# A five-layer graph kernel: half-width messages, fewer sorted supers, one-hots made two batches ahead

## The reference

```python
mean = segment_sum(h2[src], dst) / max(cnt, 1)
out  = l2norm(mean @ Wl2 + b + h2 @ Wr2)      # Wl2, Wr2: 128 x 64
out  = l2norm(out + x)
```

## Time and profile before

| what | us |
|---|---|
| median of 3 runs | 9816.29 |
| lowest, highest | 9815.36, 9822.09 |
| the profiled execution, its own time | 9828.25 |
| its span in the trace | 9826.3 |

### The profile page before, as it was taken

The page is one execution under the profiler, slowest core; times in us unless marked ns, Lnnn a source line. Parts: engine busy times, 40 slices in busy tenths (PEclk is TensorE's granted clock), DMA queues, the critical chain, the costliest instruction groups (busy, mean ns, idle before and its releaser), DMA issues.

```text
span 9826.3 us, 131949 instructions
## 1 busy us (share of the span) xinstructions
PE 5787.9 (59%) x31232; PEld 4379.0 (45%) x31233; DVE 3782.0 (38%) x8447; ACT 1893.4 (19%) x4165; POOL 6141.1 (62%) x6486
## 2 busy tenths in 40 slices
PE   4576675556666666688888236666666633333333
PEld 3444454446666666555555223434443422222222
DVE  3355552224444444455555333444444311111111
ACT  1111111111111111122222123333333300000000
POOL 6766557767777777765655324444444357777777
PEclk6555556557777777788888657778778755555555
DMA  3111111123333333355555224444444311111111
GB/s 74 34 28 27 27 27 35 35 47 98 98 97 98 98 98 97 105 136 135 135 132 131 60 84 146 142 144 150 147 149 146 106 38 30 30 30 30 30 30 29
DMA packets 544865, 813.71 MB, mean 83 GB/s; under 512 B 200060, under 2 KB 343256, under 8 KB 544010
## 3 DMA queue, kind: packets, MB, share of 16 engines
q0 software_dynamic: 207424, 296.93, 14.7%
q1 hardware_dynamic: 200459, 408.44, 13.0%
q10 hardware_dynamic: 136191, 99.81, 3.3%
HBM read 706.10 MB, written 98.49 MB: 82 GB/s over the span
## 4 chain that ended last, share of the span: by engine, by line
POOL 37%; PE 16%; issue 15%; DMA 14%; DVE 10%; SPq 5%; ACT 3%; ACTq 1%; DVEq 0%; POOLq 0%
POOL G L832 37%; PE PH L1980 9%; DMA HT<-src_rows 9%; SPq L640 3%; PE NB L1980 3%; PE PAG L1980 2%; DMA GROWS<-h_tab 2%; PE NA L1980 2%; DVE HT L1815 2%; DMA HT<-h_tab 2%; DVE HT L1747 1%; SPq L632 1%; ACTq L884 1%; DVE HT L1764 1%; SPq L742 1%
## 5 line engine op out<-in xcount | busy, mean ns | idle before, releaser
L1980 PE MATMUL PH<-HT 128*128 128x288 bf16 (+6 forms) x12902 | 2494.2, 335 | 1380.9 <-DVE HT L1815 522.9
L1980 PE MATMUL PAG<-OH,G 128*64 128x96 f32 (+2 forms) x9910 | 1519.8, 332 | 1832.9 <-DMA G<-rel_tab,IDX 986.2
L1980 PEld LDWEIGHTS PH<-HT 128*128 128x128 bf16 (+4 forms) x12902 | 1549.1, 152 | 2304.2 <-ACT HT L869 550.5
L1980 PEld LDWEIGHTS PAG<-OH,G 128*64 128x64 f32 (+2 forms) x9910 | 1393.7, 209 | 1951.8 <-issue 1904.8
L832 POOL DMA_INDIRECT G<-in_x,SRC x1525 | 1453.9, 953 | 688.2 <-issue 451.1
L832 POOL DMA_INDIRECT G<-h_tab,SRC x1040 | 984.7, 947 | 1392.0 <-PE PAG L1980 1074.8
L832 POOL DMA_INDIRECT G<-rel_tab,IDX x1507 | 1422.1, 944 | 574.6 <-issue 459.8
L832 POOL DMA_INDIRECT G<-far_tab,SRC x1527 | 1442.2, 944 | 485.0 <-issue 465.3
L1424 DVE TENSOR_TENSOR AGG<-AGG,PAG 128x96 f32 (+2 forms) x832 | 205.9, 247 | 2807.0 <-PE PAG L1980 2801.7
L832 POOL DMA_INDIRECT G<-x_tab,SRC x883 | 837.9, 949 | 534.4 <-PE PAG L1980 270.8
L1980 PE MATMUL PAG<-OH,HT 128*128 128x96 f32 x3126 | 613.3, 377 | 521.4 <-ACT HT L1120 521.4
(11 more groups left out here) (240 smaller groups left out, 4827.8 us busy)
## 6 DMA issues: line engine op xcount, KB each, us to landing
HT<-h_parts SPq DMA_DIRECT2D x150, 937.5 KB
HT<-x_parts SPq DMA_DIRECT2D x210, 468.8 KB
GROWS<-rel_tab SPq DMA_DIRECT2D x4096, 0.2 KB
HT<-src_rows SPq DMA_DIRECT2D x370, 160.0 KB
GROWS<-in_x SPq DMA_DIRECT2D x3584, 0.2 KB
rel_tab<-STG ACTq DMA_DIRECT2D x200, 250.0 KB
GROWS<-far_tab SPq DMA_DIRECT2D x3072, 0.5 KB
GROWS<-rel_tab ACTq DMA_DIRECT2D x3072, 0.2 KB
```

Source lines behind the costliest of these rows:

```text
L1980: return nc.tensor.matmul(dst, lhsT, rhs, start=start, stop=stop, skip_group_check=True)
```

## The change

**Half-width messages.** After layer 2 a pass of its own, `messages`, runs over the 50 units: SyncE loads `hT` (4 buffers), ScalarE applies batch norm and relu, TensorE multiplies by `[Wl2 | Wr2]` (128 x 128) and adds the bias, ScalarE copies the result, ScalarE stores the `Wr2` half (`r_tab`), SyncE stores the `Wl2` half (`g_tab`, 64 columns), VectorE splits that half into three bf16 parts and SyncE stores them (`g_parts`). Layer 3 gathers 64-column rows from `g_tab`, with no shift and no relu, when all stores of `g_tab` and `r_tab` have landed; a unit's first beat has two products with `FOLD` (which adds the two halves of the sums) and adds the row of `r_tab`. `h_tab`, gamma's row and the constant row `CROW_P` are gone.

**Supers.** 64 supers are sorted, over steps 60 to 188 of layer 0, a super in two steps (order and one-hots in one, ranks in the next). Layers 2 and 3 both gather 132 and pick 64 (16 windows, 160 batches), spread evenly over the first 126 steps.

**Buffers.** `PX` has 5 buffers, `SROW` 4, the source one-hots 3, the destination one-hots 4; VectorE makes one-hots two batches ahead, SyncE loads four batches ahead. The wide compare is five compares of 288 f16 columns.

```diff
-CELL_LAYERS = {2: (112, 29), 3: (132, 35)}
+CELL_LAYERS = {2: (132, 35), 3: (132, 35)}
-SORT_STEP = 40
-COUNT_SUPERS = 3 * CELL_SUPERS
+SORT_STEP = 60
+COUNT_SUPERS = 4 * CELL_SUPERS
-WIDTH = {2: PARTS * D, 3: PARTS * H}
-PAIR = {2: 2, 3: 1}
+WIDTH = PARTS * D
+PAIR = 2
-PX_BUFS = {2: 6, 3: 3}
+PX_BUFS, SROW_BUFS = 5, 4
+S_BUFS, D_BUFS = 3, 4
+HOT_AHEAD, LOAD_AHEAD = 2, 4
+HT_BUFS = 4
...
-        due = min(s + 1, head) if s < ramp else min(total, head + -(-(total - head) * (s - ramp + 1) // steps))
+        due = min(total, -(-total * (s + 1) // (supers - 6)))
```

SyncE, with the message pass between the two `load_cells`:

```diff
+            def messages():
+                def load(u):
+                    b = u % HT_BUFS
+                    if u >= HT_BUFS:
+                        sp.wait_ge(msg_hot, u - HT_BUFS + 1)
+                    sp.dma_start(HTB[:, b, :], turned(u)).then_inc(ht_in[b], 16)
+                sp.wait_ge(stored[2], all_stored(2))
+                for u in range(HT_BUFS):
+                    load(u)
+                for u in range(UNITS):
+                    sp.wait_ge(msg_copied, u + 1)
+                    sp.dma_start(rows_of(g_tab, u), MESSAGES[u % 2][0:HALF, :, 0:D]).then_inc(msg_out[u % 2], 16)
+                    if u + HT_BUFS < UNITS:
+                        load(u + HT_BUFS)
+                    sp.wait_ge(msg_split, 4 * u + 4)
+                    sp.dma_start(g_parts[0:HALF, u, :], PARTS_X[0:HALF, u % 2, :]).then_inc(g_parts_out[u % 2], 16)
...
             def load_batch(p, g):
+                b, u = g % PX_BUFS, g % BATCHES * BATCH
+                if p == 3 or g >= PX_BUFS:
+                    sp.wait_ge(cell_picked, pairs_covering(p, g - PX_BUFS))
...
+                b = g % SROW_BUFS
+                if p == 3 or g >= SROW_BUFS:
+                    sp.wait_ge(cell_hot, BATCHES_BEFORE[p] + g - SROW_BUFS + 1)
```

GpSimd before layer 3, and ScalarE:

```diff
-                        pool.wait_ge(stored[2], all_stored(2))
+                        messages_out(pool)
...
+            def messages():
+                def take(u):
+                    rows_ = MESSAGES[u % 2][0:HALF, :, :]
+                    act.wait_ge(msg_made, u + 1)
+                    if u >= 2:
+                        act.wait_ge(msg_out[u % 2], 32 * (u // 2))
+                        act.wait_ge(msg_split, 4 * (u - 1))
+                    copy(rows_, MESSAGE_P[u % 2].rearrange("p (a c) -> p a c", a=2)).then_inc(msg_copied, 1)
+                    act.wait_ge(msg_copied, u + 1)
+                    act.dma_start(rows_of(r_tab, u), rows_[:, :, D:2 * D]).then_inc(msg_out[u % 2], 16)
+                act.wait_ge(bn_ready, 1)
+                for u in range(UNITS):
+                    act.wait_ge(ht_in[u % HT_BUFS], 16 * (u // HT_BUFS + 1))
+                    if u >= 2:
+                        act.wait_ge(msg_made, u - 1)
+                    nc.scalar.activation(POS[:, u % 2 * UNIT:(u % 2 + 1) * UNIT], HTB[:, u % HT_BUFS, :], ACT.Relu,
+                                         bias=BSH[:, 0:1], scale=BSC[:, 0:1]).then_inc(msg_hot, 1)
+                    if u:
+                        take(u - 1)
+                take(LAST)
```

VectorE:

```diff
-                if 0 <= i < SORT_SUPERS:
-                    sort_hot_of(i)
-                if 0 < i <= SORT_SUPERS:
-                    sort_rank_of(i - 1)
+                if 0 <= i < 2 * SORT_SUPERS:
+                    (sort_rank_of if i % 2 else sort_hot_of)(i // 2)
...
+            def messages():
+                for u in range(UNITS):
+                    parts = PARTS_X[0:HALF, u % 2, :].rearrange("p (a c) -> p a c", a=2)
+                    rows_, left = MESSAGES[u % 2][0:HALF, :, 0:D], XS[0:HALF, :, :]
+                    dve.wait_ge(msg_copied, u + 1)
+                    if u >= 2:
+                        dve.wait_ge(g_parts_out[u % 2], 16 * (u // 2))
+                    move(parts[:, :, 0:D], rows_).then_inc(msg_split, 1)
...
+                    nc.vector.tensor_tensor(parts[:, :, 2 * D:3 * D], left, parts[:, :, D:2 * D], ALU.subtract)\
+                      .then_inc(msg_split, 1)
...
-                nc.vector.tensor_tensor(HOT_D[:, g % 3, :, :], IOTA_P.unsqueeze(1).to_broadcast(wide),
-                                        DST_TAB[:, w, u:u + BATCH].unsqueeze(2).to_broadcast(wide), ALU.is_equal)\
-                  .then_inc(cell_hot, 1)
+                for i in range(BATCH):
+                    last = nc.vector.tensor_scalar(HOT_D[:, g % D_BUFS, i, :], COLS_16[:, :], DST_TAB[:, w, u + i:u + i + 1], None,
+                                                   ALU.is_equal)
+                last.then_inc(cell_hot, 1)
...
-                        shift_straight(s, s % SLOTS)
```

TensorE:

```diff
+            def messages():
+                for u in range(UNITS):
+                    pe.wait_ge(msg_hot, u + 1)
+                    if u >= 2:
+                        pe.wait_ge(msg_copied, u - 1)
+                    bank, hot = MESSAGE_P[u % 2], u % 2 * UNIT
+                    for a in range(2):
+                        mm(bank[:, a * H:(a + 1) * H], POS[:, hot + a * HALF:hot + (a + 1) * HALF], wlr2[:, :], a == 0,
+                           False)
+                        last = mm(bank[:, a * H + D:(a + 1) * H], ONES[0:1, 0:HALF], sb2r, False, a == 1)
+                    last.then_inc(msg_made, 1)
...
-                        with_bias(NA[0:HALF, a * D:(a + 1) * D], HB[:, half(a)], wr2[:, :], sb2r)
-                        last = mm(NB[0:HALF, a * D:(a + 1) * D], Z[:, half(a)], wl2[:, :])
+                        last = mm(NB[0:HALF, a * D:(a + 1) * D], Z[:, half(a)], FOLD[:, :])
...
-                if 0 < i <= SORT_SUPERS:
-                    sort_order_of(i - 1)
-                if 1 < i <= SORT_SUPERS + 1:
-                    sort_place(i - 2)
+                if i % 2 and 0 < i < 2 * SORT_SUPERS:
+                    sort_order_of(i // 2)
+                if i % 2 == 0 and 0 < i <= 2 * SORT_SUPERS:
+                    sort_place(i // 2 - 1)
```

More of the change, by code:

```diff
@@ L776, in load_cells @@
+                    ahead = [g for at in BATCHES_AT[p][:s + 1] for g in at][-1] + LOAD_AHEAD
+                    for g in range(loaded_batches, min(ahead + 1, batches_of(p))):
+                        load_batch(p, g)
+                        loaded_batches = g + 1
                     piece = P // 8
@@ L996, in beat3 @@
                     root(3, u, 3, beat - 2)
+                    if beat == 2 and (not isinstance(u, int) or u < LAST):
+                        act.wait_ge(chain[3], u * CHAIN[3] + 1)
+                        act.dma_start(RU[0:HALF, :, :], rows_of(r_tab, unit_of(3, u + 1))).then_inc(ru_in, 16)
                 if beat == 5:
@@ L1878, in cell_layer @@
                 _, by_step, rest, _ = CELL_SCHEDULE[p]
-                m, supers = (D if p == 2 else H), SUPERS_OF[p]
+                supers = SUPERS_OF[p]
                 windows = batches_of(p) // BATCHES
@@ L2095, in sum_straight @@
                 b, landed = (None, None) if p == 1 else row_buffer(p, s)
-                if b is not None and p != 3:
+                if b is not None:
                     pe.wait_ge(row_in[b], landed)
@@ L2322, in sum_cells @@
                     pe.wait_ge(cell_copied, PAIRS_BEFORE[p] + e + 1)
[L2323 to L2324 removed]
+                    for k in range(PAIR):
+                        cell = e * PAIR + k
                         g, i = divmod(cell, BATCH)
@@ L2328, in sum_cells @@
                             pe.wait_ge(window_added, WINDOWS_BEFORE[p] + cell // UNITS)
-                        hot = HOT_D[:, g % 3, i, :]
+                        hot = HOT_D[:, g % D_BUFS, i, :]
                         rows_ = PICKED[:, e % GP_BUFS, k * w:(k + 1) * w]
-                        if p == 2:
-                            mm(WIN_SUM, rows_[:, 0:2 * D], hot, first, False)
-                            last = mm(WIN_SUM[0:D, :], rows_[:, 2 * D:3 * D], hot, False, final)
-                        else:
-                            for part in range(PARTS):
-                                last = mm(WIN_SUM, rows_[:, part * H:(part + 1) * H], hot, first and part == 0,
-                                          final and part == PARTS - 1)
+                        mm(WIN_SUM, rows_[:, 0:2 * D], hot, first, False)
+                        last = mm(WIN_SUM[0:D, :], rows_[:, 2 * D:3 * D], hot, False, final)
                     last.then_inc(cell_summed, 1)
```

383 lines of the change are left out of this document (127 added, 256 removed).

## The result

The changed kernel takes 8769.55 us (median of 4 runs, 8763.57 to 8782.85) beside 9819.19 us of the kernel before on the same chip (4 runs, 9815.36 to 9832.08): a ratio of 0.893, 95% interval 0.8915 to 0.8946. Predicted were 8660 us and a range of 8585 to 8890. The profiled execution took 8782.85 us, its span is 8781.0; so the sum of the prediction (a span of 8670) is 111 us short. Where they are is read by stage.

What follows compares the result with a forecast made beforehand. GpSimd's gathers, one per 1.249 us, were taken as every stage's floor, with 1580 us of waits to win. Terms -217 - 36 + 17 + 122 - 1042 = -1156 from a 9826.3 us span gave 8670, hence 8660; range 8585 to 8890.

Steps and rivals of the forecast that it cites:

- loop of two engines: Stage 0: VectorE's one-hots and ranks, TensorE's placing, then the unit's beat take 13.6 us a sorting step, against 9.7 of gathers.
- the 1042 us of stage 3: Stage 3: forecast gain before the message pass, from 2453.5 us to 1299 of gathers, 25 of waits and 87 at the end.
- Stage 0: Stage 0: sorting work spread over two steps, about 9.0 us a step, under the gathers' 9.7; -217 us, bounds 0 and -235.
- The compares: Stages 2 and 3: 1600 new narrow compares lengthen GpSimd's gathers by 11 ns each; +17 us over both stages.
- Rival (c): Stages 2 and 3: new compares block gathers for their whole length, 1600 x 250 ns = 400 us; 9040 us, chance 0.04.
- It is worth nothing: Five compares for one save VectorE 0.4 us a batch, with no gain because GpSimd sets the pace.
- The message pass: New pass between stages 2 and 3: 2.3 us a unit, TensorE's work the longest part; +122 us with first load and last store.
- Stage 3's waits: Stage 3: 25 us left for waits, as its eight beats a unit have more waits between engines than stage 2's five.
- rival (d): Stages 2 and 3: SyncE's queue, loads behind waits then 16 single-row DMAs, sets the pace; slower, 9975 us, chance 0.02.
- rival (a): Stages 2 and 3: TensorE and the beats set the pace, 11 us a super; 8930 us, chance 0.13.
- loads now have three to four batches of lead: Stage 2: loads get 25 us and more of lead, against waits of 16 us at the longest; 8 us of waits remain.
- The last gap: End of stage 3, before stage 4: 87 us where it was 114.8, since TensorE no longer runs behind.

## Why GpSimd waits in stage 3

The changed kernel's timeline around one such wait (SyncE's issues, then TensorE and GpSimd):

```profile
6085.11 0.26 SPq L749 DMA_DIRECT2D HT<-g_parts  x1
...
6085.42 0.35 SPq L755 DMA_DIRECT2D HT<-src_rows  x1
...
6087.98 5.12 SPq L632 DMA_DIRECT2D GROWS<-g_tab  x16
...
6093.75 2.47 PE L1921 MATMUL PAG<-OH,G 128*64 128x96 f32 x14 [8.00 <-DMA GROWS<-g_tab]
...
6096.81 0.94 POOL L833 DMA_INDIRECT G<-g_tab,SRC  x1 [4.25 <-PE PAG L1921]
```

The last of the 128 single rows of a super are issued behind the loads of a batch, which waited for a buffer. TensorE stands 8.0 us for them, then GpSimd 4.25 us for TensorE. Over the whole run:

```profile
PE PAG L1921 <- DMA GROWS<-g_tab: 114.4, 14, 14.5
DVE HT L1756 <- DMA HT<-src_rows: 110.8, 40, 11.1
```

**Rows first.**

```diff
                 for s in range(SUPERS_OF[p]):
+                    if rows_now and s:
+                        some_rows(p, s * piece, (s + 1) * piece)
                     ...
                         load_batch(p, g)
-                    if (s + 1) * piece <= P * len(SP_SUPERS[p]):
-                        some_rows(p, s * piece, (s + 1) * piece)
```

(`rows_now` is the condition of the two lines taken out; at step 0 the rows stay behind the loads.)

> The changed kernel, but in each step of stages 2 and 3 SyncE issues the 16 single-row transfers ahead of the batch loads in place of behind them. Theory A (GpSimd's 84 us of waits in stage 3 come from rows that are issued late, behind a load that waits for a free buffer): TensorE's waits for the rows fall from 114 us (14 of them) to under 30, GpSimd's waits for sums in stage 3 from 84 to under 30 us, and the stage gets 40-60 us shorter; stage 2 changes by less than 15 us. Theory B (TensorE itself is late in stage 3, and the rows are only where it shows): GpSimd's waits stay between 70 and 100 us and another wait takes the rows' place. A third way: the batch loads now come late, and VectorE waits for source rows; then stage 3 gets longer.

**The lookahead of before.**

```diff
-PX_BUFS, SROW_BUFS = 5, 4
-S_BUFS, D_BUFS = 3, 4
-HOT_AHEAD, LOAD_AHEAD = 2, 4
+PX_BUFS, SROW_BUFS = 5, 2
+S_BUFS, D_BUFS = 2, 3
+HOT_AHEAD, LOAD_AHEAD = 1, 2
```

> The changed kernel with the lookahead of before: one-hots one batch ahead (not two), loads two (not four), two buffers for source rows (not four), two for source one-hots (not three), three for destination one-hots (not four). Five buffers of parts stay. The prediction gave the lookahead the credit for the loads' slack. If that is right, VectorE waits for source rows for some 200-400 us again (678 before, 111 in the changed kernel) and GpSimd's waits for sums grow in stages 2 and 3 from 85 us to 200-500 us. If the narrower messages alone did it (a batch of 3.6 us of TensorE's work where it had 6.0), the span grows by less than 40 us.

With the rows first the span was 8746.6 us, 34 less than the changed kernel, nearly all of it in stage 3 (1362.0 us for 1394.1). What waits were left in stage 3, and over the run those for single rows and for source rows:

```profile
POOL G L836 <- PE PAG L1924: 57.9, 22, 9.1
...
PE PAG L1924 <- DMA GROWS<-g_tab: 1.5, 1, 1.5
...
DVE HT L1759 <- DMA HT<-src_rows: 197.6, 69, 10.7
```

TensorE's waits for the rows went from 114.4 us (14) to 1.5 (1), but GpSimd's only from 83.9 to 57.9. Between the two theories: the rows were one cause, of 26 to 34 us; the rest stays when they are on time. TensorE is busy for 166 of the 200 us from 6400 to 6600 in that run, but VectorE now waits 198 us for source rows (111 in the changed kernel), and its later work waits behind that. The runs of the section on a version of the parts speak against TensorE's own work as the cause of the last 58 us: with rows first, the bias on VectorE and one-hots one batch ahead in stage 3, GpSimd waits 18.6 and 25.3 us there, while TensorE's busy time is nearly the same (1095 and 1082 us, 1104 here). With one-hots still two batches ahead (and the wide compare) it waits 66.2. So most of the 58 us most likely belongs to one-hots that are made too early, a part of the change itself; that step was not tried by itself.

The shorter lookahead cost nothing. The span was 8749.0, stage 2 12.8 us shorter (1324.9, outside the spread) and stage 3 16.0 (1378.1, hardly outside it), although VectorE waited for source rows 275 us in place of 111:

```profile
DVE HT L1756 <- DMA HT<-src_rows: 274.8, 92, 11.1
```

So two buffers are enough in the changed kernel, and the extra ones are not what made it faster. (The expectation's 3.6 us of TensorE's work a batch is one stretch; the means of stage 3 are 4.7 us a batch now and 6.6 before.) In stage 3 TensorE's waits for single rows fell to 12.6 us, as fewer loads stand ahead of them, so a part of its 16 us is likely the effect of the run before. Why stage 2 came out shorter, and not equal, is open: it is in its gathers (970 ns mean for 983, 43 of them over 1.1 us for 69). It is not the one-hots one batch ahead alone: with these and loads four ahead, below, the mean is 992.

## Where stage 0's gain comes from

**A whole super a step again**, with 64 sorted supers:

```diff
-                if 0 <= i < 2 * SORT_SUPERS:
-                    (sort_rank_of if i % 2 else sort_hot_of)(i // 2)
+                if 0 <= i < SORT_SUPERS:
+                    sort_hot_of(i)
+                if 0 < i <= SORT_SUPERS:
+                    sort_rank_of(i - 1)
```

(and TensorE's and ScalarE's parts of a step likewise).

> The changed kernel, still with 64 supers sorted, but one whole super is sorted in each step of stage 0 again (one-hots and ranks of VectorE and the placing of TensorE in the same step) in place of half of that work per step. If the loop of the two engines was what held up stage 0, GpSimd's waits for sums there go from 15 us to 64 x 2.8 = 180 us (234.7 us for 84 such steps before), and the stage from 1949 to 2100-2130 us; stages 1 to 4 stay. If stage 0 got shorter mainly because 20 fewer supers are sorted, the waits stay under 60 us.

```profile
L833 POOL DMA_INDIRECT G<-in_x,SRC x1525 | 1450.3, 951 | 630.9 <-issue 454.3 <-PE PAG L1923 174.2 <-DMA SRC<-in_src_c 2.4
```

GpSimd waits 174.2 us again, 2.7 a sorted super as before (234.7 / 84 = 2.8), and stage 0 takes 2077.9 us from first gather to last for 1927.2. Of the gain of 213 us, 151 are from spreading a super over two steps and some 60 from the 20 supers that are not sorted (20 x 2.8 = 56). The prediction's loop of two engines stands.

## What paces the message pass

A unit takes 2.65 us (stores of `g_parts` from 5271.2 to 5401.2, 49 steps of 2.653). One unit in the changed kernel's timeline:

```profile
5299.39 0.68 PE L1921 MATMUL PH<-rows,ONES 1*125 1x64 f32 x2
...
5299.99 0.79 PE L1921 MATMUL PH<-wlr,POS 128*125 128x128 f32 x2
...
5300.71 0.68 PE L1921 MATMUL PH<-rows,ONES 1*125 1x64 f32 x2
...
5300.94 0.25 SPq L741 DMA_DIRECT2D g_parts<-HT  x1
...
5301.32 0.79 PE L1921 MATMUL PH<-wlr,POS 128*125 128x128 f32 x2
...
5302.04 0.68 PE L1921 MATMUL PH<-rows,ONES 1*125 1x64 f32 x2
...
5304.93 0.23 DVE L1471 TENSOR_SCALAR HT<-Y 125x128 bf16<-125x128 f32 x1 [1.45 <-DMA g_parts<-HT]
```

TensorE runs back to back: a product every 0.72 us, a bias row 0.61, twice each, 2.66 us. But VectorE also waits in 23 of the 50 units, for the store of two units before (issued 5300.94, its buffer used again at 5304.93). Two candidates with almost the same length; three runs tell them apart.

**The bias moved** to VectorE in stage 3, which has room:

```diff
-                        mm(bank[...], POS[...], wlr2[:, :], a == 0, False)
-                        last = mm(bank[:, a * H + D:(a + 1) * H], ONES[0:1, 0:HALF], sb2r, False, a == 1)
+                        last = mm(bank[...], POS[...], wlr2[:, :], a == 0, a == 1)
...
+                    run(nc.vector.tensor_tensor(Y[0:HALF, :, 0:D], Y[0:HALF, :, 0:D], SB2[...], ALU.add))
```

> The changed kernel, but the bias of layer 2's second convolution is no longer added by TensorE in the message pass (two one-row matmuls a unit, 0.61 us each) but by VectorE in stage 3 (one more 125x128 add a unit, of some 0.3 us). Theory A (TensorE alone sets the pace of the message pass): a unit falls from 2.65 us to 1.45-1.8 us, and the gap before stage 3 from 190.5 us to 130-150. Theory B (a loop of almost the same length lies right behind it: VectorE's four steps, the store of the parts and its landing, with two buffers, 5.16 us for two units): the unit stays at 2.5-2.65 us and the gap within 10 us of 190. Stage 3's gathers stay as they are under both.

**Three buffers.**

```diff
-        MESSAGES = [Y, Y2]
+        MESSAGES = [Y, Y2, STG[:, 1, 0:2 * H].rearrange("p (a c) -> p a c", a=2)]
-        PARTS_X = half_words(o, 2, 2 * WIDTH, BF16)
+        PARTS_X = half_words(o, 3, 2 * WIDTH, BF16)
```

> The changed kernel, the bias moved to VectorE in stage 3 as in the run before, and also three buffers in place of two for the message pass's results (messages and their parts) on their way to memory. With the bias moved alone, a unit still took 2.58 us or so, because VectorE and ScalarE waited for the stores of two units before to land. Theory A (that landing is a latency): a third buffer takes it out; ScalarE's copy, issue and relu (some 1.7 us) and TensorE's 1.3 to 1.45 us are next, a unit takes 1.8-2.1 us and the gap before stage 3 falls from 188-191 us to 150-165. Theory B (the DMA engines or memory are the limit, at the 130 GB/s that the pass has now): the landing gets as much longer as more stores are under way, the unit stays at 2.4 us or more and the gap over 178 us.

**Another queue** for the loads:

```diff
-                    sp.dma_start(HTB[:, b, :], turned(u)).then_inc(ht_in[b], 16)
+                    act.dma_start(HTB[:, u % HT_BUFS, :], turned(u)).then_inc(ht_in[u % HT_BUFS], 16)
```

> The kernel with the bias on VectorE and three buffers in the message pass, whose unit took 2.5-2.6 us with the landing of a load up from 4.1 to 5.6 us at 135-145 GB/s; now ScalarE issues the pass's loads (125 KB a unit) in place of SyncE, so that SyncE's queue carries 156 KB a unit and ScalarE's 187 KB, where they carried 281 and 62. Theory A (what limits the pass is how fast one queue's transfers go): the rate rises to 165-200 GB/s, a unit takes 1.7-2.1 us and the gap before stage 3 falls from 187.7 to 145-168 us. Theory B (the DMA engines, busy for 45-50% by the profile, or memory limit these small rows whatever the queue): the rate stays at 135-145 GB/s, the unit at 2.4-2.6 us and the gap over 180 us.

| run | us a unit | gap before stage 3 | landing of a load, us | GB/s, 5310 to 5360 |
|---|---|---|---|---|
| changed kernel | 2.65 | 190.5 | 4.1 | 133 |
| bias moved | 2.60 | 186.7 | 4.5 | 135 |
| and three buffers | 2.57 | 186.8 | 5.6 | 136 |
| and loads by ScalarE | 2.56 | 187.4 | 5.8 | 135 |

The stretch from 5310 to 5360 in the changed kernel, and in the run with three buffers:

```profile
5310.00:5360.00 50.00, 50.00 (x152) 37.21 (x152) 19.73 (x76) 18.39 (x38) 0.00 (x0) 0.50 0.50 133
```

```profile
5310.00:5360.00 50.00, 23.11 (x76) 17.46 (x76) 19.99 (x77) 16.70 (x39) 0.00 (x0) 0.50 0.50 136
```

TensorE's work halves (50.0 to 23.1 us of 50) and the pass does not get shorter. A third buffer only makes each transfer land later, at the same rate. Nor is it SyncE's queue: with the loads on ScalarE's, the rate is the same 135 GB/s. So the pass moves 352,000 bytes a unit (128,000 of `hT`, 96,000 of parts, 64,000 of each half) at some 135 GB/s, which is 2.6 us a unit, and no run brought it below 2.56. In the changed kernel TensorE's 2.66 us a unit are the longer of the two by less than 0.1 us. That one queue is not the limit agrees with the Trainium skill (DMA: Bandwidth & Descriptors, Issuing engines are not separate DMA queues), by which a second issuing engine saves the time to issue and nothing more. What below the queues limits it (the DMA engines are at 0.50 by the profile; rows of 256 to 1000 bytes) was not tried apart.

## A version of the parts

The rows first, the bias on VectorE, three buffers and the wide compare in both stages:

> All that seemed to help, on the changed kernel: the single wide compare for destinations, single-row transfers ahead of the batch loads, the bias on VectorE, and three buffers in the message pass. If the parts add up: stage 2 -21 us, message pass -30 to -40, stage 3 -34 (rows) and +14 (wide compare), so a span of 8695-8715 us where the changed kernel had 8781. If the wide compare and the rows first together make VectorE wait for source rows and TensorE for VectorE in stage 3, that stage takes over 1395 us from first gather to last, and the span is over 8730.

The same with the narrow compares and one-hots one batch ahead:

> As the run before, but with the five narrow compares kept and the one-hots made one batch ahead in place of two (loads stay four ahead). One batch ahead with loads two ahead took 13 us from stage 2 and 16 us from stage 3 of the changed kernel. If the gains add: stage 2 1325 us, stage 3 1345-1362 us, message pass -30 to -40 us, a span of 8685-8705 us. If the gain of the shorter lookahead came from the later loads and not from the one-hots, stages 2 and 3 stay at 1339 and 1362 and the span is 8705-8720.

The spans were 8732.7 and 8737.5 us: both missed. A large part of the miss is the message pass, for which 30 to 40 us had been expected before the run with three buffers was made; it gave 4 and 6. With the wide compare, stage 2 took 1314.6 and stage 3 1367.4 us, 23 and 27 less than the changed kernel (21 and 20 expected). With the narrow ones one batch ahead, stage 3 took 1347.7 us and GpSimd waited there for 18.6 us only, but stage 2 took 1347.8: its gathers had a mean of 992 ns, the most of any run. GpSimd's idle time before the gathers of stage 3 (us, times), first with the wide compare, then with the narrow ones one batch ahead:

```profile
  PE PAG L1928: 66.2, 21
...
  PE PAG L1928: 18.6, 10
```

Each is better in one stage, which is what the section on the gathers would say: GpSimd's time counts in stage 2, VectorE's in stage 3. The last run takes each where it helped, with the rows first and the bias on VectorE, and two buffers in the pass again:

```diff
-HOT_AHEAD, LOAD_AHEAD = 2, 4
+HOT_AHEAD, LOAD_AHEAD = {2: 2, 3: 1}, 4
...
+                if p == 2:
+                    nc.vector.tensor_tensor(HOT_D[:, g % D_BUFS, :, :], ..., ALU.is_equal).then_inc(cell_hot, 1)
+                    return
                 for i in range(BATCH):
```

> The parts that helped, each where it helped: the single wide compare in stage 2 only (there GpSimd sets the pace and a gather held up costs time), the five narrow compares and one batch of lookahead in stage 3 only (there TensorE is late and VectorE's time counts), single-row transfers ahead of the batch loads in both, the bias on VectorE; two buffers in the message pass, as the third brought nothing. If each stage keeps what it showed: stage 2 1315-1318 us from first gather to last (1337.7 in the changed kernel), the gap before stage 3 187-189 (191.5), stage 3 1346-1362 us (1394.1), so a span of 8705-8725 us, below the changed kernel's 8781 and the 8733 of all parts in both stages. If the short lookahead and the wide compare only did well through chance positions of the loads, stage 3 stays over 1365 us and the span over 8730.

```profile
L838 POOL DMA_INDIRECT G<-g_tab,SRC x1040 | 1015.2, 976 | 525.5 <-issue 500.2 <-PE PAG L1934 25.3
L838 POOL DMA_INDIRECT G<-x_tab,SRC x1040 | 995.9, 958 | 334.7 <-issue 316.5 <-DMA x_tab<-XS 17.8 <-PE PAG L1934 0.3
```

It takes 8715.72 us (median of 5 runs, 8707.41 to 8731.48), 0.887 of the kernel before, interval 0.8858 to 0.8885, which does not touch the changed kernel's 0.8915 to 0.8946. Stage 2 took 1311.9 us, the gap 187.9 (from start to start of the gathers, as the expectation counts it), stage 3 1352.8, the span 8711.1: as expected, but for stage 2, 3 us better. It is a run of all these parts together; what each is worth in it is known only from the single runs. GpSimd's waits in stage 3 are 25.3 us; its gathers there still lose 33 us to the narrow compares.

## Why the prediction was right, and where it was off

- **Direction, place and size** held: of 1580 us of waits for `PAG` 100 are left, TensorE's work a super is 7.7 and 8.3 us (forecast 7.7 and 8.2), a floor of one gather per 1.249 us reached in stages 0 and 2 but for the longer gathers, 1040 gathers in stage 2. The time lay within the range, 110 us above the forecast, and 10 us outside the forecast's own range (8590 to 8760). What is argued and not tried: no run takes back the half-width messages, or the 132 gathered supers of stage 2, by themselves, so how the 1042 us of stage 3 divide between narrower batches, the missing shift and relu, and the earlier one-hots rests on the sums.
- **Stage 0**, -217: measured -213, one wait of 14.9 us for the 18 left for waits, and undoing the spreading gives 2.7 us a super back.
- **The compares**, +17, "now and then one may hold up the other, but the means say it is rare": the term that was mis-sized most for its size. It measured +60. Two steps failed. The 1600 new compares cost 31 us, 19 ns each for the 11 taken. And the sum put the source compares at nothing (it took 944 ns a gather), where they hold the other 29. A price of a compare does not carry over from one kernel to the next: in stage 2 two source compares ahead of one wide compare cost 10 ns each before (4.4 us, 420 of them) and 59 ns each in the changed kernel with the wide compare (19.0 us, 320 of them), the same instructions in the same order. What differs there (GpSimd waits 0.9 us for 271, the order of steps is new) was not tried apart. The maxima that the prediction saw (1348 and 644 ns) were the sign that a single meeting can be dear, though the means were small. And taking all of it away gives 36 us in stage 2 and nothing in all. Rival (c), 400 us for the whole length of every new compare, was far off too.
- **"It is worth nothing"** (VectorE's time) holds in stage 2 and not in stage 3: 0.5, 1.1 and 1.3 us more a batch made stage 3 longer by 15, 21 and 36 us.
- **The message pass**, 2.3 us a unit by TensorE's work, was 2.65, and the gap 19 us longer. The sum had the right engine and too low a price: TensorE's products and bias rows take 2.66 us at a clock of 0.50, where 1.8 to 2.4 were taken. What it did not price at all are the transfers, which hold a unit at 2.56 to 2.60 us when TensorE's work is halved. That TensorE was the bound in the changed kernel is a matter of 0.1 us, so even a right price for it would have been right partly by luck.
- **Stage 3's waits**, 25 us, were 84. "Eight beats a unit have more waits of one engine for another" was the wrong place for a third or more of them: they were single rows issued behind the batch loads in SyncE's queue. The part of rival (d) that reads "16 single-row DMAs, in one order" was right as a mechanism and small as a price. Of the other 58 us, most went away with one-hots made one batch ahead (18.6 and 25.3 us left, other parts changed with it), at nearly the same busy time of TensorE; so rival (a), TensorE's work, is at most a small part, and not 273.
- **The lookahead** got the credit for "loads now have three to four batches of lead". Half of that lead is as good or better. What made room is then among the rest of the change: narrower batches (in stage 3), fewer batches a super (in stage 2), their even spread and shorter destination compares. Which of these was not tried.
- **The last gap**, 87 us, was 89.5.

## What to carry to other kernels

When an engine that sets the pace has a mean above its median, look at what runs beside its longest instructions before anything else: a wait is on record, a longer instruction is not. A cost of interference that is a mean over meetings holds for the kernel in which it was read: here the same pair of compares went from 10 to 59 ns each. Ask of each microsecond on a helper engine which stage it falls in; the same compare is free where GpSimd leads, and costs time where GpSimd waits for sums. And price a pass over memory by its bytes at the rate that the trace shows for rows of that size, even where an engine's work seems to fill it.

## What the runs showed of the hardware

- TensorE's clock stood at 0.50 (its lower level, 1.2 GHz) for the whole message pass of the changed kernel, though it was busy for 50.0 of 50 us from 5310 to 5360; in the last 53 us of stage 2's gathers it was busy for 20.65 us, with a clock of 0.56, and in the next 53 for 30.0 at 0.50. What would have raised it was not tried.
- Narrow compares of 16-bit data in SBUF lengthen some of the gathers beside them, and are at times lengthened too: the 14 compares of 288 columns that met no gather took 286 to 291 ns, the median of all 1600 was 282, the longest 515; the gathers' longest in stage 2 was 3.3 us for a median of 0.94. The same compare from f32 in PSUM took 504 ns with a spread of 495 to 519, and the gathers' excess in that run, 29 us over both stages, was the same as with one wide compare from PSUM.
- Transfers of rows of 256 to 1000 bytes ran at 133 to 136 GB/s with the DMA engines at 0.50, with two or three stores under way and over one queue or two.
